# Row normalisations as one GpSimd instruction each, quantiser scales on GpSimd, wide copies and squares on ScalarE, and new orders of work

## The reference

```python
# layer 0: cross attention over channels, 8 heads of 8 channels, rotary, softmax over 256 positions
q, k, v = proj(layernorm(x)), proj(ctx), proj(ctx)
x1 = x + Wo @ softmax(rope(q) @ rope(k).T / sqrt(8)) @ v
# layer 0: gated FFN with fake-quantised (8 bit) rows and ternary weights, 256 -> 1024 -> 256
h  = silu(bitlinear(layernorm(x1), gate_w)) * bitlinear(layernorm(x1), val_w)
x2 = x1 + bitlinear(h, out_w)
# layer 1: one-head attention of 64 rows over the 64 context rows, masked
x3 = x2 + softmax(layernorm(x2) @ ctx.T / 16 + mask) @ ctx
# layer 1: gated FFN, ternary groups of 64 weights, 256 -> 1024 -> 256, the hidden row scaled by its RMS
x4 = x3 + rms_norm(silu(g) * u) @ p_w.T
```

## Time and profile before

| what | value |
|---|---|
| median of 3 runs | 828.62 us (824.5 to 832.47) |
| span of the profiled execution | 828.8 us |
| PE busy | 759.6 us (92%) |
| DVE busy | 739.1 us (89%) |
| ACT busy | 699.6 us (84%) |
| POOL busy | 636.2 us (77%) |
| instructions on DVE, ACT, POOL | 1636, 1447, 1139 |

### The profile page before, as it was taken

The page is one execution under the profiler, slowest core; times in us unless marked ns, Lnnn a source line. Parts: engine busy times, 40 slices in busy tenths (PEclk is TensorE's granted clock), DMA queues, the critical chain, the costliest instruction groups (busy, mean ns, idle before and its releaser), DMA issues. The chain is left out here.

```text
span 828.8 us, 22129 instructions
## 1 busy us (share of the span) xinstructions
PE 759.6 (92%) x6898; PEld 397.6 (48%) x6898; DVE 739.1 (89%) x1636; ACT 699.6 (84%) x1447; POOL 636.2 (77%) x1139
## 2 busy tenths in 40 slices
PE   2588999999999999999999999999999999998876
PEld 1233344444455554555555555555554545444444
DVE  3898798999999999999999999999999999987765
ACT  3788987988899898999898989999998888887644
POOL 3765656778898888988888888888888887777632
PEclk9555898999999999999999999999999999999999
DMA  8410222344434444544445444444444445434230
GB/s 287 140 54 19 71 67 64 76 105 94 112 87 108 109 110 110 108 116 112 104 111 116 112 101 110 109 105 106 117 101 120 99 91 115 95 87 91 57 72 20
DMA packets 197952, 82.59 MB, mean 100 GB/s; under 512 B 139710, under 2 KB 196670, under 8 KB 197836
## 3 DMA queue, kind: packets, MB, share of 16 engines
q1 hardware_dynamic: 193260, 74.63, 38.5%
q10 hardware_dynamic: 4576, 6.55, 2.4%
...
...
## 5 line engine op out<-in xcount | busy, mean ns | idle before, releaser
L1141 DVE TENSOR_REDUCE mx<-psS 128x2 f32<-128x512 f32 x512 | 334.1, 680 | 21.8 <-PE psS L630 20.2
L813 ACT ACTIVATE prob<-psT 128x512 f32<-128x512 f32 x512 | 292.5, 604 | 27.0 <-PE psT L638 21.6
L630 PE MATMUL psS<-KQ 31*128 31x256 f16 x1024 | 137.6, 285 | 7.0 <-DVE mx L1141 3.6
L652 PE MATMUL psW<-prob,vst 128*32 128x256 f32 x2048 | 143.0, 400 | 0.1
L741 PE MATMUL psW<-guT,xT 128*128 128x512 bf16 x512 | 132.6, 387 | 6.2 <-DMA xT<-stage 5.3
L638 PE MATMUL psT<-KQ 32*128 32x256 f16 x1024 | 130.4, 280 | 4.0 <-ACT prob L813 3.1
L652 PEld LDWEIGHTS psW<-prob,vst 128*32 128x32 f32 x2048 | 55.0, 112 | 61.4 <-issue 34.6
L741 PEld LDWEIGHTS psW<-guT,xT 128*128 128x128 f16 x512 | 43.1, 99 | 71.5 <-issue 36.5
L1025 POOL TENSOR_TENSOR hqB<-wide,rnd 128x512 bf16<-128x512 f32 x60 | 63.1, 1056 | 13.6 <-ACT wide L863 13.4
L1039 POOL TENSOR_TENSOR stage<-stage 128x512 f16<-128x512 f32 x60 | 69.7, 1162 | 2.5 <-ACT stage L924 1.8
L630 PEld LDWEIGHTS psS<-KQ 31*128 31x128 f16 x1024 | 40.4, 93 | 64.2 <-DVE mx L1141 38.0
...
## 6 DMA issues: line engine op xcount, KB each, us to landing
KQ<-hl SPq DMA_DIRECT2D x192, 64.0 KB, 1.9
...
```

The lines of the kernel that those rows point to most:

```text
L630: m = nc.tensor.matmul(psS[:, n % 2, T * k:T * k + T], KQ[p % DEEP][r, 1, g, 128 * k:128 * k + 128], KQ[p % DEEP][r, 0, g, :], start=True, ...
L652: m = nc.tensor.matmul(bank[32 * j:32 * j + 32, :], vst[p % DEEP][:, k, 4 * n + j, :], prob[:, (4 * n + j) % 8, k, :], start=(k == 0), sto ...
L813: m = nc.scalar.activation(flat(prob[:, n % 8, :, :]), psT[:, n % 2, :], ACT.Exp, scale=float(HC) ** -0.5)
L1141: m = nc.vector.tensor_reduce(mx[:, p % 2, :, 4 * (n % 4) + n // 4], psS[:, n % 2, :].rearrange("p (c s) -> p c s", c=NK), AX.X, ALU.max)
```

## The change

**Normalisations.** `xnB`, `xnD` and `xnC` become one instruction on POOL each, a `tensor_scalar` that subtracts the mean and multiplies by the reciprocal deviation, both read from a column. The tiles `ceB`, `ceD`, `ceC` and the wait between the two go.

**Scales.** `sxB` and `sx` move from DVE's queue to POOL's. The reciprocals become powers of -1 there. `amB` and `amH` wait for the scale step of two pairs before.

**Stage C.** `hh` and `sq` work on all 1024 columns at once, so `sq` has one accumulator read; both wait for the second half of `hC`. `ms` loses the addition and takes its product and sum in one `tensor_scalar`. The semaphores of `hC`, `hl` follow.

**Orders.** All five tables are new, in head, loop and tail. The loop's counter is shifted (the step `S` is written `:-2` where it was `:0`), which by itself moves nothing, and the distances between the stages of a pair are counted in the same number of pairs: `x4` is seven pairs behind `mx` in both.

```diff
-INNER = {"xnB": 1, "xnD": 1, "xnC": 1, "rsP": 2, "rsB": 1, "rsC": 1, "rsD": 1, "sxB": 1,
-         "sx": 2, "ms": 3, "rs": 1, "rq": 3, "rn": 1, "fr": 1, "ra": 3, "fx": 1, "gv": 4,
+INNER = {"rsP": 2, "rsB": 1, "rsC": 1, "rsD": 1, "sxB": 1,
+         "sx": 2, "ms": 1, "rs": 1, "rq": 3, "rn": 1, "fr": 1, "ra": 3, "fx": 1, "gv": 4,
...
-    "dve": """mx6:0 x4:-7 bsP:3 x3:-5 mx7:0 bsC:-5 fx2:-4 mx8:0 mx9:0 ct0:-2 ct1:-2 mvC:-5 cl1:0 r1:2 mx10:0 mx11:0
...
+    "dve": """mx0:-2 mx1:-2 aC0:-8 amB:-5 mx2:-2 aC1:-8 mx3:-2 wx:-7 mx4:-2 bsP:1 mvP:1 hC0:-8 mx5:-2 hC1:-8 rc:-4 mx6:-2 mx7:-2
...
                 elif kind == "sq":
-                    after(act, "hC", p, n)
+                    after(act, "hC", p, 1)
                     after(act, "ms", p - 1)
-                    m = nc.scalar.activation(sqC[:, n, :], hC[:, n, :], ACT.Square, accum_out=ssq[:, n:n + 1])
+                    m = nc.scalar.activation(flat(sqC), flat(hC), ACT.Square, accum_out=ssq[:])
                 elif kind == "hh":
-                    after(act, "hC", p, n)
+                    after(act, "hC", p, 1)
                     after_late(act, p - 1, "lz", "hT", part=1)
-                    m = nc.scalar.copy(hhl[:, 0, n, :], hC[:, n, :])
+                    m = nc.scalar.copy(flat(hhl[:, 0, :, :]), flat(hC))
...
-                    centre = {"xnB": ceB, "xnD": ceD, "xnC": ceC}[kind]
                     after(pool, ready, p)
-                    inner(1, nc.gpsimd.tensor_tensor(centre[:], src[:], mv[:, 0:1].broadcast_to([P, T]),
-                                                     ALU.subtract))
                     after(pool, last_use, p - 1, part)
                     if kind == "xnC":
                         after(pool, "xl", p - 1)
-                    m = nc.gpsimd.tensor_tensor(dst[:], centre[:], rs[:, 1:2].broadcast_to([P, T]), ALU.mult)
+                    m = nc.gpsimd.tensor_scalar(dst[:], src[:], mv[:, 0:1], rs[:, 1:2], ALU.subtract, ALU.mult)
+                elif kind == "sxB":
+                    if p == 0:
+                        after(pool, "gv", 0)
+                    after(pool, "amB", p)
+                    after(pool, "xr", p - 2)
+                    after(pool, "rq", p - 2)
+                    after(pool, "tB", p - 2, 1)
+                    after(pool, "sx", p - 2)
+                    sc = sB[:, p % 2, :]
+                    inner(1, nc.gpsimd.tensor_scalar(sc[:, 1:2], sc[:, 0:1], 1e-5, 1.0 / 127.0, ALU.max, ALU.mult))
+                    nc.gpsimd.tensor_scalar(sc[:, 4:5], sc[:, 1:2], gam_q[:, 0:1], None, ALU.mult)
+                    nc.gpsimd.tensor_scalar(sc[:, 5:6], sc[:, 1:2], sc[:, 1:2], gam_q[:, 1:2], ALU.mult, ALU.mult)
+                    m = nc.gpsimd.tensor_tensor(sc[:, 2:3], sc[:, 1:2], mone[:], ALU.pow)
+                elif kind == "sx":
+                    sc = sB[:, p % 2, :]
+                    after(pool, "amH", p)
+                    after(pool, "hr", p - 2, 1)
+                    after(pool, "x2", p - 2)
+                    inner(1, nc.gpsimd.tensor_scalar(sc[:, 6:7], sc[:, 3:4], sc[:, 5:6], 1e-5, ALU.mult, ALU.max))
+                    inner(2, nc.gpsimd.tensor_tensor(sc[:, 7:8], sc[:, 6:7], mone[:], ALU.pow))
+                    nc.gpsimd.tensor_scalar(sc[:, 9:10], sc[:, 6:7], gam_q[:, 2:3], None, ALU.mult)
+                    m = nc.gpsimd.tensor_scalar(sc[:, 8:9], sc[:, 7:8], sc[:, 5:6], 127.0, ALU.mult, ALU.mult)
...
-                    after(pool, "sq", p, 1)
+                    after(pool, "sq", p)
                     after(pool, "x4", p - 2)
-                    inner(1, nc.gpsimd.tensor_tensor(sc[:, 0:1], ssq[:, 0:1], ssq[:, 1:2], ALU.add))
-                    inner(2, nc.gpsimd.tensor_tensor(sc[:, 1:2], sc[:, 0:1], eps[:, 1:2], ALU.mult))
-                    inner(3, nc.gpsimd.tensor_tensor(sc[:, 3:4], sc[:, 1:2], hsc[:, 2:3], ALU.add))
-                    m = nc.gpsimd.tensor_tensor(sc[:, 2:3], sc[:, 3:4], mhalf[:], ALU.pow)
+                    inner(1, nc.gpsimd.tensor_scalar(sc[:, 0:1], ssq[:], 1.0 / HID, hsc[:, 2:3], ALU.mult, ALU.add))
+                    m = nc.gpsimd.tensor_tensor(sc[:, 1:2], sc[:, 0:1], mhalf[:], ALU.pow)
...
                     if kind == "amB":
                         after(dve, "xnB", p)
+                        after(dve, "sxB", p - 2)
                     else:
                         after(dve, "hB", p, 1)
+                        after(dve, "sx", p - 2)
...
-                elif kind == "sxB":
-                    after(dve, "amB", p)
...
-                    m = nc.vector.reciprocal(sc[:, 2:3], sc[:, 1:2])
...
-                elif kind == "sx":
...
-                    m = nc.vector.tensor_scalar(sc[:, 8:9], sc[:, 7:8], sc[:, 5:6], 127.0, ALU.mult, ALU.mult)
```

More of the change, by code:

```diff
@@ new lines @@
+    "act": """E15:-4 pc:-1 th0:-8 xnP:0 th1:-8 xcTc:-7 E0:-3 hr0:-6 u1:-4 E1:-3 hr1:-6 xr:-5 vst:-1 xq:-5 pD:-7 E2:-3 E3:-3 pTc:-7
+           E4:-3 hh:-8 E5:-3 E6:-3 hi:-1 E7:-3 sq:-8 E8:-3 tB0:-5 u0:-3 E9:-3 E10:-3 xh:-7 E11:-3 E12:-3 tB1:-5
+           x1:-4 E13:-3 mxc:-2 md:-2 E14:-3""",
+    "pool": """rsP:1 hl0:-8 lo:-1 rsC:-7 xnC:-7 om:-4 ms:-8 xl:-7 hl1:-8 rsD:-6 xb:-4 xnD:-6 rsB:-4 xnB:-4 sx:-5 r2:0 sxB:-4 hq0:-5
+           rq:-4 hq1:-5 rs:-6 rot:0""",
+    "sp": """or:-4 cB:-6 kq:-1 xT:-7 hT:-8 xP:2 st:-9 xA:-3 sg:-3 ov:-3 cP:1 qT:-4 d1:-3 ht:-5""",
@@ new lines @@
+    "pool": """rsP:0 id:0 r2:0 rot:0 lo:0 rsP:1 qa0:0 r2:1 rot:1 rsP:2 qa1:0 lo:1 qb0:0 r2:2 rot:2 rsP:3 qa2:0 lo:2 qb1:0 rsP:4
+           r2:3 rot:3 lo:3 qb2:0 om:0 rsB:0 xnB:0 rsP:5 sxB:0 r2:4 rq:0 rot:4 lo:4 om:1 xb:0 rsP:6 rsB:1 xnB:1 sx:0
+           sxB:1 hq0:0 rq:1 r2:5 hq1:0 rot:5 rsP:7 om:2 lo:5 xb:1 rsD:0 xnD:0 rsB:2 xnB:2 sxB:2 r2:6 sx:1 rq:2 rs:0
+           xb:2 rot:6 hq0:1 hq1:1 rsC:0 lo:6 om:3 xnC:0 xl:0 rsB:3 xnB:3 sxB:3 rsD:1 rq:3 rsP:8 xnD:1 r2:7 sx:2 rs:1
+           hq0:2 rot:7 hq1:2 xb:3 rsC:1 lo:7 om:4 xnC:1 hl0:0 xl:1 hl1:0 rsD:2 xnD:2 r2:8 rsB:4 xnB:4 rsP:9 sxB:4
+           rot:8 rq:4 sx:3 rs:2 ms:0 xb:4 lo:8 hq0:3 hq1:3 hl0:1 om:5 rsC:2 xnC:2 hl1:1 rsP:10 xl:2 xb:5 ms:1 rsD:3
+           xnD:3 rsB:5 xnB:5 sx:4 r2:9 sxB:5 hq0:4 rq:5 hq1:4 rs:3 rot:9""",
@@ L935, in _ @@
             nc.gpsimd.memset(mhalf[:], -0.5).then_inc(S["set_pool"], 1)
[L936 to L937 removed]
+            nc.gpsimd.memset(eps[:], EPS_LN).then_inc(S["set_pool"], 1)
             nc.gpsimd.memset(rnd[:], ROUND).then_inc(S["set_pool"], 1)
```

403 lines of the change are left out of this document (188 added, 215 removed).

## The result

The changed kernel takes 881.32 us, the median of 4 runs (874.77 to 886.17), against 828.05 for the kernel before beside it: a ratio of 1.062, 95% interval 1.054 to 1.069. I had predicted 804 with a range up to 836. The profiled execution spans 881.3 us.

The account below looks back on a forecast made before the run. PE and DVE were taken to hold each other through two-deep buffers. A pair falls from 22.41 to 21.4 us, the loop by 26.9, filling and draining add 2: 828.8 - 26.9 + 2 = 803.9, called 804, range 784 to 836.

Parts of the forecast that it names:

- PE's own work: PE's time per pair without stalls: taken as 20.4 us, up to 21.71 if the weight-load waits are hidden.
- the longer way of the scales over POOL: Chain amH, sx, hr across three engines instead of two: costed at nothing in the loop.
- the 1.0 I expected to win: Gain per pair in the loop: from 22.41 to 21.4 us, 1.0 us less.
- the waits for `mx`: PE's weight loads waiting for `mx` on DVE, 17.5 us before: cut by half or more if the forecast is right.
- The first, PE as its own bound: PE's work is 21.7 us a pair, its waits hidden behind matmuls; only some 0.5 us goes: 817 us, chance 0.20.
- a DVE idle for 10%: Sign of PE as its own bound: DVE idle at 10% with PE's busy time unchanged at 21.7 us a pair.
- The third, "the orders give it back": New DVE-POOL hand-overs and POOL's strict queue add waits of 0.8 us a pair on PE's path: 826 us, chance 0.16.
- POOL's price: One-instruction normalisation of 256 columns on POOL: 0.47 us each, 1.41 for three, POOL's busy time 19.4 us a pair.
- the upper bound: No gain over the two old normalisation passes on POOL: 1.24 us an instruction, POOL at 21.7 us a pair.
- the fourth rival: POOL becomes the bound through the new `tensor_scalar`: at 1.24 us a pair takes 23.3, 854 us; chance 0.10.
- 1.56 us a pair: The eight instructions of `sxB` and `sx` leave DVE, 1564 ns a pair: DVE from 21.39 to about 19.8 us.
- The wide instructions: Copies and squares of 1024 columns on ACT: 1055 and 1060 ns, saving 0.64 us a pair, ACT from 20.31 to 19.7.

Follow-up runs that it names:

- the isolated price: Kernel before with six patterns of score and wide matmuls appended to PE's queue: each further group of scores cost 0.42 us; the run took 935.89 us.
- the first two experiments: Changed kernel with scale steps sx and sxB back on DVE, 887.38 us; changed kernel with xnB, xnD and xnC on DVE instead, 891.23 us.

## Why the prediction was wrong

**The step that failed is PE's own work.** I took "20.4 for PE's own work", bounded it by 21.7, and carried both over to the changed kernel. PE's new table has no term in the sum; what I costed at nothing "since the distances in pairs are kept" was the longer way of the scales over POOL. PE is busy 23.55 us a pair now, 1.84 more, and the union of the scores grew by 1.90, from 4.23 to 6.13 us a pair in the 500 us. Less all waits of the weight loads it is 21.66, 1.3 above the 20.4. PE's work is not the sum of its matmuls but depends on their order, which the earlier trace rows can't show; the two tables of PE do, and I had not compared them for runs. By the isolated price the estimate would have been (16.0 - 11.1) x 0.42 = 2.1 us a pair on PE (measured: 1.84), against the 1.0 I expected to win. Of the waits for `mx`, which were to be cut by half or more, more came: 17.5 us became 25.2.

**Of the rivals none had it.** The first, PE as its own bound, was right that PE sets the pair, and its sign of a DVE idle for 10% came true (53 of 500 us); but it had PE's work unchanged at 21.7. The third, "the orders give it back", looked at the new orders, but was meant as hand-overs between DVE and POOL, at most 22 us. Those hand-overs are well placed in the new tables.

**POOL's price was mis-sized, and came out at the upper bound.** The groups by shape of the changed kernel (`xnD` and `xnC` have 1226 and 1245):

```profile
L994 POOL TENSOR_SCALAR xnB<-x,mvB,rsB 128x256 f32<-128x256 f32 x30 | 36.7, 1222 | 2.7
```

1.23 us instead of 0.47. The row of 2 partitions by 128 columns, from which I took 0.76 ns a column, is in bf16 and on two partitions, and said nothing of 128 partitions in f32. The Trainium skill's 1.03 cycles per element for a body of at most two operations (GPSIMD Engine Reference, section 3.1) does not hold for this instruction: 3.3 ns a column are 4.0 of its cycles of 1.2 GHz. POOL's busy time, 21.72 us a pair, is the 21.7 that I gave for this bound, in part by luck: the six `tensor_scalar` of one column in `sxB` and `sx` took 268 to 336 ns, where I had 267 at most. The conclusion of the fourth rival, that POOL then sets the pair, fell with the first two experiments: it is 23.67 us with POOL busy for 459 us of 500 and 23.60 with 403. That the rival's 23.3 for the pair lies near is chance.

**DVE lost less than its durations.** I subtracted 1.56 us a pair. Between the one with the scales back on DVE and the changed kernel, DVE's busy time differs by 464.58 / 21.19 - 447.00 / 21.13 = 0.77 us a pair. In the records an instruction often starts before the one ahead of it ends (busy time is a union), so the sum of the durations is more than what they occupy. From 21.39 a pair DVE fell to 21.16, not to 19.8. The other DVE instructions of a pair, summed one by one, are the same (23.3 us before, 23.5 after), but their union rose from 20.35 to 21.16: they overlap less. That this is because DVE now waits for PE between them (18.9 us, 5.7 before) fits, but was not tested.

**The wide instructions were sized well.** 1055 and 1060 ns expected:

```profile
L923 ACT ACTIVATE stage<-stage 128x1024 f16<-128x1024 f32 x32 | 33.7, 1053 | 0.0
L927 ACT CAST stage<-stage 128x1024 f16<-128x1024 f32 x32 | 33.4, 1043 | 3.0 <-DVE stage L1274 3.0
```

But ACT's busy time fell only from 20.31 to 20.18 us a pair, not to 19.7, and while ACT isn't the bound that is worth nothing. In the old orders waiting for the second half cost 15 us, where I had put up to 0.3 us a pair, 8 in the loop.

**What stays open.** The 0.42 us explains 45 of the 53 us; the other 8 were not separated, nor how much of the 45 falls in the draining, which is 11 us longer. The new orders with the old instruction forms were not run, nor the new table of PE alone, so what the forms and the other four tables win or lose inside the changed kernel is not known. That the new tables with large groups would be faster than before was not shown: no such table was found by simple rules.
